# Spectral block mixing of a 4x128x128x768 image on one core: TensorE's loop unrolled by five, and three changes beside it

## What is computed

```python
xf = jnp.fft.rfft2(x, axes=(1, 2), norm='ortho')           # (4, 128, 65, 8, 96), complex
o1r = relu(xr @ w1[0] - xi @ w1[1] + b1[0])                # 96x96 matrices for each block
o1i = relu(xi @ w1[0] + xr @ w1[1] + b1[1])
o2r = softshrink(o1r @ w2[0] - o1i @ w2[1] + b2[0], 0.01)
o2i = softshrink(o1i @ w2[0] + o1r @ w2[1] + b2[1], 0.01)
out = jnp.fft.irfft2(o2r + 1j * o2i, s=(128, 128), axes=(1, 2), norm='ortho') + x
```

## Time and profile before

| | |
|---|---|
| median of three runs | 4975.89 us |
| the profiled execution | 4975.77 us |
| its span | 4973.7 us |
| mean granted TensorE clock | 0.989 of full |
| TensorE matmul busy | 4779.5 us, 96% of the span |
| VectorE, ScalarE, GpSimd busy | 4070.3, 2514.4 and 1028.1 us |
| DMA | 421 MB, 85 GB/s over the span |

### The profile page before, as it was taken

The page is one execution under the profiler, slowest core; times in us unless marked ns, Lnnn a source line. Parts: engine busy times, 40 slices in busy tenths (PEclk is TensorE's granted clock), DMA queues, the critical chain, the costliest instruction groups (busy, mean ns, idle before and its releaser), DMA issues.

```text
span 4973.7 us, 120408 instructions
## 1 busy us (share of the span) xinstructions
PE 4779.5 (96%) x44930; PEld 3997.2 (80%) x44930; DVE 4070.3 (82%) x6763; ACT 2514.4 (51%) x4290; POOL 1028.1 (21%) x836
## 2 busy tenths in 40 slices
PE   6999999999999999999999999999999999999997
PEld 5888888888888887888878788788888888788886
DVE  5888888888888888888888888788887888888876
ACT  4554455545555445555445554455544555445553
POOL 0220222211222112222022220122211222102222
PEclk9999999999999999999999999999999999999999
DMA  6422544324443234442344423444224453234522
GB/s 110 102 60 51 107 104 104 77 45 95 103 103 87 43 86 103 103 99 44 74 103 103 108 50 62 101 103 108 63 61 88 103 108 78 59 76 103 107 53 51
DMA packets 1079029, 421.33 MB, mean 85 GB/s; under 512 B 1076128, under 2 KB 1076256, under 8 KB 1078432
## 3 DMA queue, kind: packets, MB, share of 16 engines
q1 hardware_dynamic: 1073696, 411.61, 39.1%
q10 hardware_dynamic: 4736, 1.60, 0.1%
HBM read 210.19 MB, written 201.33 MB: 83 GB/s over the span
## 4 chain that ended last, share of the span: by engine, by line
PE 85%; DVE 6%; issue 5%; ACT 3%; POOL 1%; SPq 0%; ACTq 0%; DMA 0%; DVEq 0%; POOLq 0%
PE ps L515 14%; PE ps L611 13%; PE ps L493 10%; PE ps L536 10%; PE ps L620 6%; PE ps L548 5%; PE ps L594 5%; PE ps L582 4%; PE ps L646 3%; PE ps L561 3%; PE ps L569 2%; PE ps L562 2%; ACT rings L733 2%; DVE ydg L954 1%; DVE biased L929 1%
## 5 line engine op out<-in xcount | busy, mean ns | idle before, releaser
L1051 POOL TENSOR_TENSOR whole<-whole 128x480 f32<-128x480 f32 (+1 forms) x416 | 499.4, 1200 | 3904.0 <-DVE whole L979 3904.0
L743 ACT COPY ydg<-ps 128x512 f32<-128x512 f32 (+4 forms) x1024 | 588.3, 578 | 571.4 <-PE ps L494 352.9
L611 PE MATMUL ps<-wts,hbig 128*128 128x192 f32 x4160 | 735.1, 328 | 4.3
L493 PEld LDWEIGHTS ps<-tab,rings 128*64 128x64 f32 x6144 | 675.3, 138 | 78.8 <-ACT rings L733 42.7
L493 PE MATMUL ps<-tab,rings 128*64 128x128 f32 x6144 | 701.2, 275 | 35.1 <-ACT rings L733 34.2
L515 PE MATMUL ps<-tab,rings 128*128 128x128 f32 x6144 | 712.1, 280 | 15.9 <-DVE rings L949 15.9
L515 PEld LDWEIGHTS ps<-tab,rings 128*128 128x128 f32 x6144 | 708.0, 196 | 18.8 <-DVE rings L949 17.9
L494 PE MATMUL ps<-tab,rings 128*63 128x128 f32 x6144 | 701.4, 275 | 0.0
L611 PEld LDWEIGHTS ps<-wts,hbig 128*128 128x128 f32 x4160 | 672.1, 190 | 20.6 <-ACT hbig L791 13.7
L494 PEld LDWEIGHTS ps<-tab,rings 128*63 128x63 f32 x6144 | 675.0, 137 | 0.0
L929 DVE TENSOR_TENSOR biased<-ps,wts 128x768 f32<-128x768 f32 (+1 forms) x544 | 498.9, 917 | 194.0 <-PE ps L620 189.4
(11 more groups left out here) (82 smaller groups left out, 8893.8 us busy)
## 6 DMA issues: line engine op xcount, KB each, us to landing
out<-whole SPq DMA_DIRECT2D x704, 240.0 KB, 4.2
whole<-in_x SPq DMA_DIRECT2D x384, 384.0 KB, 6.5
whole<-in_x SPq DMA_DIRECT2D x64, 408.0 KB, 7.8
whole<-in_x SPq DMA_DIRECT2D x64, 360.0 KB, 6.7
out<-whole SPq DMA_DIRECT2D x64, 216.0 KB, 3.5
wts<-in_mix SPq DMA_DIRECT2D x16, 513.0 KB, 4.9
out<-whole SPq DMA_DIRECT2D x64, 120.0 KB, 3.2
out<-whole SPq DMA_DIRECT2D x64, 96.0 KB, 2.9
```

The lines of the kernel that those rows point to most:

```text
L493: pe.matmul(o[0:HALF], slot[:, 0:HALF], mat("fwd_w"), start=True, stop=True)
L611: mm = pe.matmul(o, hbig[:, k * H:(k + 1) * H], mix_part("w2_big"), start=first, stop=False, skip_group_check=True)
L743: act.copy(*line_moves(stage, g)).then_inc(line_act, 1)
L1051: pool.tensor_tensor(xs[p][:, a:b, :], u, xm, ALU.add).then_inc(y_plus, 1)
```

## The change

In four parts: TensorE's loop has three rounds of five steps each. ScalarE's `move_row0` goes from the end of the step into the forward lines, ahead of group 6, and waits for `uv_ready` of the whole pass before (all `add_halves` done); the wait for `v_done` and `u_done` is gone, and ScalarE's loop now closes after it has packed five groups. In the same part the waits for GpSimd's groups are split: `round_small` waits for groups 0-1, VectorE's `remainder` for 0-5, the first `relu` for 0-7, `shrink` as before. The odd columns of slab 0 are loaded by ScalarE's queue, the even ones by SyncE's. In the last pass GpSimd does groups 0 to 5 and VectorE, after its last `add_halves`, groups 6 to 12. Small memsets go to a tile of their own (`scrap`).

```diff
+POOL_LAST = 6
+MOVE_ROW0_AT = 6
+UNROLL = 5
...
+        def piece_rows(i):
+            a, e = i * LOAD_ROWS, (i + 1) * LOAD_ROWS
+            return (a, e + (e == HALF)), (H + 1 - e, H + 1 - max(a, 1))
...
-                load_x(0, 0, 0)
+                for i in range(PIECES):
+                    load_piece(0, 0, 0, i, (0,))
                 sp.dma_start(tab[:, FWD:TABLE], table[:, FWD:TABLE]).then_inc(table_loaded, 16)
...
-                with pe.Fori(0, STEPS - 1) as t:
-                    step(t, False)
+                with pe.Fori(0, (STEPS - 1) // UNROLL) as rounds:
+                    for i in range(UNROLL):
+                        step(rounds * UNROLL + i, False)
                 step(STEPS - 1, True)
...
                 def lines(q, p, stage):
                     for g in range(NG):
+                        if stage == 0 and g == MOVE_ROW0_AT:
+                            move_row0(q)
...
                 def move_row0(q):
+                    act.wait_ge(uv_ready, NF * q + NF)
                     act.wait_ge(row0_copied, q + 1)
...
                 def copy_big(q, u, h):
-                    if u == 0 and h == 0:
-                        wait_batch(act, q - 1, NF - 1)
...
                 def round_small(q, u):
+                    if u == 0:
+                        wait_batch(act, q - 1, 1)
...
                     act.wait_ge(big_mixed, NU * q + u + 1)
-                    if u:
+                    if u == 0:
+                        wait_batch(act, q - 1, 7)
+                    else:
                         act.wait_ge(hbig_read, NU * q + u)
...
                                 pack_lines(q + 1, 1 - p, g)
-                            act.wait_ge(v_done, NF * q + NF)
-                            act.wait_ge(u_done, NF * q + NF)
-                            move_row0(q + 1)
-
+                first = x[0:1, :, :, 0:CB].rearrange("o h (m t) c -> (o t) m h c", t=2)
+                for i in range(PIECES):
+                    for lo, hi in piece_rows(i):
+                        act.dma_start(xs[0][HALF:W, lo:hi, :], first[1, :, lo:hi, :]).then_inc(x_loaded[0][i], 16)
...
-                move_row0(0)
...
                     dve.wait_ge(zsmall_hi_ready, NU * q + u + 1)
+                    if u == 0:
+                        wait_batch(dve, q - 1, 4)
...
+                def last_sums(q, p, g):
+                    a, b = odd_rows(g)
+                    u, xm = ucopy[g][:, 0:b - a, :], mirror(xs[p], a, b)
+                    dve.wait_ge(uv_ready, NF * q + NF + g + 1)
+                    dve.tensor_tensor(xs[p][:, a:b, :], u, xm, ALU.add).then_inc(last_plus, 1)
+                    dve.wait_ge(last_plus, g - POOL_LAST + 1)
+                    dve.tensor_tensor(xm, u, xm, ALU.subtract).then_inc(batch_ready[batch_of(g)], batch_part(g))
...
                         for g in range(NF):
                             add_halves(q, p, g)
+                        if not fold_next:
+                            for g in range(POOL_LAST, NF):
+                                last_sums(q, p, g)
...
-                        for g in range(NF):
+                        for g in range(POOL_LAST if last and p == PAIRS - 1 else NF):
...
-                with pool.Fori(0, STEPS) as t:
-                    step(t)
+                with pool.Fori(0, STEPS - 1) as t:
+                    step(t, False)
+                step(STEPS - 1, True)
```

More of the change, by code:

```diff
@@ L217, in build @@
         wts = sb("wts", [128, MIXED])
+        scrap = sb("scrap", [128, 16])
         w1hi = sb("w1hi", [128, 3 * BIG], F32R)
@@ L273, in build @@
         y_plus = sem("y_plus")
+        last_plus = sem("last_plus")
         batch_ready = [sem(f"batch_ready{i}") for i in range(len(STORE_AFTER))]
@@ L412, in _, with load_piece @@
                 sp.dma_start(tab[:, 0:FWD], table[:, 0:FWD]).then_inc(fwd_loaded, 16)
-                def load_piece(n, b, p, i):
+                def load_piece(n, b, p, i, parts=(0, 1)):
                     src = x[bass.ds(b, 1), :, :, bass.ds(n * CB, CB)].rearrange("o h (m t) c -> (o t) m h c", t=2)
-                    a, e = i * LOAD_ROWS, (i + 1) * LOAD_ROWS
-                    for lo, hi in ((a, e + (e == HALF)), (H + 1 - e, H + 1 - max(a, 1))):
-                        for t in range(2):
+                    for lo, hi in piece_rows(i):
+                        for t in parts:
                             sp.dma_start(xs[p][t * HALF:(t + 1) * HALF, lo:hi, :],
@@ L1007, in step @@
                         else:
-                            dve.memset(clamped[0:1, 0:1], 0.0).then_inc(pairs_folded, FOLDS)
+                            dve.memset(scrap[0:1, 0:1], 0.0).then_inc(pairs_folded, FOLDS)
                         for it in range(2, NU + 2):
@@ L1024, in _ @@
                 dve.memset(yedge[:], 0.0).then_inc(cleared, 1)
-                dve.memset(clamped[0:1, 0:1], 0.0).then_inc(uv_ready, NF)
-                dve.memset(clamped[0:1, 1:2], 0.0).then_inc(y_plus, NF)
+                dve.memset(scrap[0:1, 0:1], 0.0).then_inc(uv_ready, NF)
+                dve.memset(scrap[0:1, 1:2], 0.0).then_inc(y_plus, NF)
                 for i, ready in enumerate(batch_ready):
-                    dve.memset(clamped[0:1, 2 + i:3 + i], 0.0).then_inc(ready, 2)
+                    dve.memset(scrap[0:1, 2 + i:3 + i], 0.0).then_inc(ready, 2)
                 dve.wait_ge(uv_ready, NF)
@@ L1043, in _, with step @@
             def _(pool):
-                def step(t):
+                def step(t, last):
                     for p in range(PAIRS):
                         q = t * PAIRS + p
-                        for g in range(NF):
+                        for g in range(POOL_LAST if last and p == PAIRS - 1 else NF):
                             a, b = odd_rows(g)
```

## The result

The changed kernel takes **4865.56 us** (median of four runs, 4864.89 to 4867.12). The kernel before, run beside it, takes 4976.67 (4975.51 to 4979.08). The ratio is 0.9776, with a 95% interval of 0.9761 to 0.979: 111 us less. The forecast was 4898.0 with a range from 4874 to 4921.

A forecast was written before the change was run, and what follows sets the result against it. The prediction took TensorE's stream plus losses at two places of each step as the bound; -48 - 44.7 + 20 - 1 - 0 - 4 = -77.7 us against 4975.77 gave 4898 us, range 4874 to 4921.

The forecast's parts named there:

- TensorE's loop: Step ends where TensorE's loop closes: 12 of 14 back branches go, 4.0 us each, 48 us less.
- The rival that the unrolled code brings gaps of its own: Between TensorE's unrolled steps: fetch gaps show all the same, the 48 us stay, 4946 us; chance 0.05.
- ScalarE's branch: Forward stages behind ScalarE's loop branch: branch hidden in the inverse W transform, 14 x 3.19 = 44.7 us less.
- Row 0, sent later: Row 0's two DMAs amid ScalarE's forward stage: TensorE waits 0.65 us in 31 passes, 20 us more.
- a lead of 1.0 us: Forward stage: ScalarE's pack of group 11 ahead of TensorE's need, 0.6 us plus 0.4 from group 0 moved sooner.
- row 0 costs nothing: Rival, forward stage: ScalarE is ahead enough, so row 0's DMAs cost 0 instead of 20 us, 4878 us; chance 0.14.
- The rival of the held-up issue: Forward stage: row 0's two issues take 1.8 us each under store load, 87 us more, 4965 us; chance 0.07.
- The first slab: Loading slab 0 over two queues: DMA engines already full at 219 GB/s, so 0 us gained; at most 10 us.
- The split waits: Start of the mixing: ScalarE's first copy no longer waits for all GpSimd groups, 1 us less, between 0 and 1.5.
- The tail: End of the last pass: last sums shared with VectorE, stores limiting at 250 GB/s, 4 us less, 1.5 to 8.4.
- faster load: Rival, slab 0: two queues load faster by up to 10 us, 4888 us; chance 0.12.

## Why the prediction was wrong, step by step

**TensorE's loop: right.** Predicted 48 us, found 45 in the times of the loop alone and 48.6 in its trace. The 46.4 of the changed kernel hold a loss of 1.8 by the split waits. What was to be late next, VectorE's L949, is what holds the start now, and the clock stays up behind it (21.70 instead of 22.79 us for the lines; over the whole span the granted clock is 0.997, where it was 0.989). The rival that the unrolled code brings gaps of its own fell twice, with five steps and with 16.

**ScalarE's branch: right.** Predicted 44.7, found 46.9. ScalarE's packs (timeline of after) are done at 328.43:

```profile
323.31 5.12 ACT L743 COPY rings<-whole 128x508 f32<-128x508 f32 x5
```

TensorE's first forward line is at 335.16, so 6.7 us lie there for a branch of 4.0. After, the stage takes 22.06 us from its first line to the mixing, where the earlier trace rows show 25.29 (timeline, then chain of waits, of after):

```profile
335.16 0.32 PE L502 MATMUL ps<-tab,rings 128*64 128x128 f32 x1
```

```profile
357.22 2.05 PE ps L545 x16
```

**Row 0, sent later: the step that failed.** The prediction set "0.53 + 0.84 us and the gaps, 195.51 to 196.91 = 1.4 us" against a lead of 1.0 us, as if the engine stood still while its queue issues. ScalarE's timeline of after, at the same place of the stage:

```profile
336.30 0.59 ACT L755 COPY ydg<-ps 127x512 f32<-127x512 f32 x1 [7.87 <-PE ps L503]
...
339.30 1.09 ACT L755 COPY ydg<-ps 127x512 f32<-127x512 f32 x2
340.13 0.53 ACTq L769 DMA_DIRECT2D ydg<-row  x1
340.26 1.14 ACT L743 COPY rings<-whole 128x508 f32<-128x508 f32 x1
340.70 0.64 ACTq L770 DMA_DIRECT2D yedge<-row  x1
341.27 1.12 ACT L743 COPY rings<-whole 128x508 f32<-128x508 f32 x1
342.26 0.62 ACT L755 COPY ydg<-ps 127x512 f32<-127x512 f32 x1
342.74 3.15 ACT L743 COPY rings<-whole 128x508 f32<-128x508 f32 x3
```

Both DMAs are issued, from 340.13 to 341.34, beside two packs, and from the stage's second copy on none shows an idle time before it. From that first move to pack 11, the first of the three, ScalarE takes 6.44 us here (336.30 to 342.74) and 6.44 us in the earlier trace rows (197.02 to 203.46), where no DMA stands in between. So the issue cost nothing at all. The lead was as predicted: pack 11 begins 7.58 us after the stage's first line, 0.45 sooner than before. The issuing time is ScalarE's queue's; it costs the engine something only when the work handed over before runs out. In the earlier trace rows it showed because the engine had been idle for 8.28 us and nothing had been handed over: a row from an idle stage gave the price for a full one. The cover is 2.3 us, two DMAs need 1.2, and six need 4.4 and cost 1.4 us a pass. So the rival "row 0 costs nothing" was right about the time, though not for the reason given there, a longer lead. The rival of the held-up issue had the right mechanism for a longer issue: it is what the four added DMAs showed. Here the two took 0.53 and 0.64 us, not the 1.8 each that it needed. The Trainium skill (Advanced Engine Details and Errata, Engine Queue Depths) gives ScalarE's queue a depth of 8. The trace agrees that there is one, and shows two copies' worth of it at this place; what kept it from more isn't shown.

**The first slab: the second step that failed.** The prediction read a DMA share of 1.31 as full engines and took "a second queue has nothing to give". The share counts the time of packets that overlap, and it fell while the rate rose by half. Averaged over the packets of 384 bytes that begin between 5 and 20 us, one took 35.9 ns on one queue, 23.2 on two with halves, and 27.7 on two split by rows. What they spend most of their time on can't be seen in these traces, but one queue does not use the engines up. The range for this term reached to 10 us, so the gain was inside its own bounds; the chance was too low. The rule weighed in the prediction, of the Trainium skill (DMA: Bandwidth & Descriptors, Rules for kernel authors), that transfers to disjoint partition halves serialize and aren't worth splitting, does not hold for this load: 324 GB/s against 221 in the same window. The slab's last packet begins at 23.7 us instead of 32.0, and of these 8.4 us TensorE got 8.1; VectorE's last folds still stand between the two.

**The split waits: mis-sized.** Predicted 1, found about 5 by stages and 4.1 when taken back. It was read from TensorE's own share in one wait of before, 1.5 us. Two things lay outside it. The wait grows when the forward stages get shorter: splitting it makes the mixing 1.5 us shorter in all in the kernel before, and 2.8 in the changed one. And the inverse lines of the passes with odd numbers start sooner behind the last `mix2_rows`, after 2.32 us instead of 2.52, 3 us in all, in both kernels alike.

**The prologue: left out.** Row 0's DMAs no longer stand ahead of the first forward lines, 28.5 to 26.5 us; with row 0 moved alone it was 26.7.

**The tail: mis-sized by 1.6 us.** Sharing the sums works as said. GpSimd's last sum and VectorE's first two, in the timelines of after:

```profile
4839.46 1.20 POOL L1078 TENSOR_TENSOR whole<-whole 128x480 f32<-128x480 f32 x1
4840.74 1.49 POOL L1080 TENSOR_TENSOR whole<-whole 128x480 f32<-128x480 f32 x1
```

```profile
4840.17 1.00 DVE L1001 TENSOR_TENSOR whole<-whole 128x480 f32<-128x480 f32 x1
4841.21 1.53 DVE L1003 TENSOR_TENSOR whole<-whole 128x480 f32<-128x480 f32 x1
4842.67 0.64 DVE L1001 TENSOR_TENSOR whole<-whole 128x480 f32<-128x480 f32 x1
...
4849.62 0.56 DVE L1003 TENSOR_TENSOR whole<-whole 128x384 f32<-128x384 f32 x1
```

VectorE is through at 4850.18, 9.9 us after its last `add_halves` (9.7 predicted). But the prediction let the stores run at 250 GB/s from 1 us after GpSimd is done with its share, which is 4842.23 here. Until then they ran at that rate; behind it they fall to about half, and are back only from 4845 on:

```profile
4840.00:4842.23 2.23, 0.00 (x0) 0.00 (x0) 2.19 (x3) 0.00 (x0) 2.15 (x2) 0.61 0.96 252
4842.23:4845.00 2.77, 0.00 (x0) 0.00 (x0) 2.70 (x5) 0.00 (x0) 0.00 (x0) 0.50 0.56 133
4845.00:4850.00 5.00, 0.00 (x0) 0.00 (x0) 4.79 (x9) 0.00 (x0) 0.00 (x0) 0.50 0.97 252
```

The missing 117 GB/s over 2.77 us are 0.32 MB, 1.3 us, where the prediction allowed 1 us to start. GpSimd's share also ended 2.0 us behind the last `add_halves`, not 1.7. These are 0.6 of the 1.6 us; the rest isn't accounted for.

**The range.** The four terms in which the time fell below the forecast (row 0, the slab, the split waits, the prologue) come to 20 + 8 + 4 + 2 = 34 us. The prediction held "row 0 free" and "faster load" for rivals, of which one comes at a time, with its low end at one of them and a little of the other. They are independent terms of one sum, and both came in.

## What to carry to other kernels

A DMA issued on an engine's queue is not a hole in that engine's work as long as enough of it has been handed over before; look for idle time of the engine behind the issue, and place such an issue where the engine is full, not where it is waiting. A hardware branch costs its gap only where nobody has work in hand: put it behind work done ahead, as ScalarE's here, or share it among several rounds, as TensorE's. Rivals on different resources are terms that can all come at once, and a range has to hold their sum.

## What the runs showed of the hardware

- **Two queues carry small packets faster than one.** Loads in 384-byte packets went from 221 GB/s on one queue to 324 over SyncE's and ScalarE's queues with half of the partitions each, and to 277 when each queue spans all of them; stores went from 246 to 289.
- **DMA share is no measure of fullness.** It was 1.31 at 211 to 221 GB/s and 1.17 at 324.
- **VectorE's sums beside GpSimd's.** VectorE's sum of 480 elements takes 0.64 us by itself, but 1.00 and 1.53 while GpSimd's run. Both end 0.51 us after a sum of GpSimd's ends (4840.66 and 4842.23), as if they had stood still until then. The Trainium skill (SBUF — State Buffer, Who interferes with whom) says that VectorE's instructions with two inputs in SBUF and GpSimd's that read it shut each other out of a shared port for a whole instruction; these rows agree. GpSimd's last sum, 1.49 instead of 1.20 us, fits as well: it began at 4840.74, when VectorE's first was still running, until 4841.17.
- **A taken branch of a long loop** left TensorE idle for 2.7 to 3.1 us in the kernel before (14 times, 2.79 on average), and all 16 steps as straight code cost no gap.
